# A vision block on one core: in its last stage, ACT scales the down product, POOL adds the residual and rounds the tokens, DVE multiplies the steps

## The reference, cut to what matters

```
def bitlinear(x, W, b):
    w_scale = clip(mean(abs(W)), EPS)
    Wq = clip(round(W / w_scale), -1, 1) * w_scale
    x_scale = clip(max(abs(x), axis=-1), EPS)          # one for each token
    xq = clip(round(x * (127 / x_scale)), -128, 127) * (x_scale / 127)
    return xq @ Wq.T + b
h = h + attention(layernorm(h))
h = h + bitlinear(gelu(bitlinear(layernorm(h), W1, b1)), W2, b2)
```

## Time and profile before

| what | us |
|---|---|
| median of 3 runs (354.68 to 358.23) | 355.41 |
| the profiled execution itself | 358.58 |
| its span, first to last instruction | 356.8 |
| PE busy | 310.9 (87%) |
| DVE busy | 247.1 (69%) |
| ACT busy | 214.6 (60%) |
| POOL busy | 136.8 (38%) |

### The profile page before, as it was taken

The page is one execution under the profiler, slowest core; times in us unless marked ns, Lnnn a source line. Parts: engine busy times, 40 slices in busy tenths (PEclk is TensorE's granted clock), DMA queues, the critical chain, the costliest instruction groups (busy, mean ns, idle before and its releaser), DMA issues.

```text
span 356.8 us, 9434 instructions
## 1 busy us (share of the span) xinstructions
PE 310.9 (87%) x3582; PEld 235.8 (66%) x3590; DVE 247.1 (69%) x647; ACT 214.6 (60%) x385; POOL 136.8 (38%) x262
## 2 busy tenths in 40 slices
PE   7385767999999999799799999999976899999884
PEld 6274656777777765465488778778754677776553
DVE  2616647677566736245558787788758999999982
ACT  2224445447576453344556665665635999999992
POOL 1215453556545524444392000000035566555630
PEclk9878999999999999899989999999999999999998
DMA  7952991000000000001311121221100001000011
GB/s 230 264 187 88 376 322 33 3 17 33 16 16 32 17 18 17 31 31 49 72 38 40 42 50 39 45 45 40 25 3 1 2 24 38 29 31 29 30 46 51
DMA packets 19291, 22.30 MB, mean 63 GB/s; under 512 B 2304, under 2 KB 15888, under 8 KB 19248
## 3 DMA queue, kind: packets, MB, share of 16 engines
q1 hardware_dynamic: 18544, 20.89, 19.5%
q10 hardware_dynamic: 704, 0.82, 0.9%
HBM read 16.68 MB, written 5.02 MB: 61 GB/s over the span
## 4 chain that ended last, share of the span: by engine, by line
PE 62%; DVE 19%; ACT 8%; issue 5%; DMA 3%; POOL 2%; SPq 0%; DVEq 0%; ACTq 0%
PE ps L400 14%; PE ps L443 10%; PE ps L524 9%; PE ps L547 7%; DVE sc L900 7%; PE ps L421 4%; DVE ximg L921 4%; PE ps L514 4%; PE ps L390 3%; DMA ximg<-in_x 3%; PE ps L532 3%; ACT ximg L1124 3%; PE ps L383 2%; PE ps L451 2%; ACT ximg L1119 2%
## 5 line engine op out<-in xcount | busy, mean ns | idle before, releaser
L1158 POOL TENSOR_TENSOR rs<-rs,nhalf 128x1 f32<-128x1 f32 (+1 forms) x76 | 41.7, 556 | 181.4 <-DVE rs L894 100.5
L400 PE MATMUL ps<-w_in,xT 128*128 128x256 f32 (+1 forms) x228 | 56.6, 401 | 5.8 <-ACT xT L986 5.8
L400 PEld LDWEIGHTS ps<-w_in,xT 128*128 128x128 f32 (+1 forms) x228 | 43.9, 200 | 12.9 <-ACT xT L986 6.3
L1076 ACT ACTIVATE ximg<-ps 128x296 f32<-128x296 f32 x64 | 26.6, 418 | 31.4 <-PE ps L524 30.8
L443 PE MATMUL ps<-w_qk,hnT 128*128 128x512 f32 (+1 forms) x76 | 37.3, 615 | 2.3 <-DVE h L703 2.3
L775 DVE TENSOR_TENSOR qa<-ps,tab 128x512 f32<-128x512 f32 (+1 forms) x19 | 13.1, 691 | 36.9 <-PE ps L383 36.9
L838 DVE TENSOR_REDUCE ximg<-ps 128x16 f32<-128x592 f32 x32 | 24.7, 773 | 16.5 <-PE ps L514 16.4
L524 PE MATMUL ps<-tab,ximg 128*128 128x128 f32 x256 | 35.7, 283 | 0.0
L1165 POOL TENSOR_TENSOR qa<-qa,qb 128x512 f32<-128x512 f32 (+1 forms) x19 | 24.1, 1267 | 15.6 <-DVE qb L783 15.6
L524 PEld LDWEIGHTS ps<-tab,ximg 128*128 128x128 f32 x256 | 28.1, 143 | 1.3
L986 ACT ACTIVATE xT<-ps 128x768 f32<-128x768 f32 (+1 forms) x19 | 15.0, 791 | 22.4 <-PE ps L390 18.6
(11 more groups left out here) (107 smaller groups left out, 673.8 us busy)
## 6 DMA issues: line engine op xcount, KB each, us to landing
ximg<-in_x SPq DMA_DIRECT2D x18, 384.0 KB, 8.0
ximg<-vsc SPq DMA_DIRECT2D x64, 51.0 KB, 2.0
vsc<-vt SPq DMA_DIRECT2D x18, 136.0 KB, 1.7
out<-ximg SPq DMA_DIRECT2D x18, 128.0 KB, 1.7
ximg<-in_W SPq DMA_DIRECT2D x2, 1024.0 KB, 10.5
qkT<-in_W SPq DMA_DIRECT2D x2, 384.0 KB, 6.2
wide<-in_rows SPq DMA_DIRECT2D x1, 640.0 KB, 5.5
w_qk<-in_Wqk SPq DMA_DIRECT2D x1, 512.0 KB, 8.6
```

Source lines behind the costliest of these rows:

```text
L400: pe.matmul(dst[0:n, :], xT[t % 2][:, k, 0:n], w_in[:, k, :], start=(k == 0), stop=False)
L1076: act.activation(pT[p % 2][:, g0:g0 + 4, :, :], ps_pT(b), ACT.Copy).then_inc(S[f"p_evac{b}"], 1)
L1158: pool.tensor_tensor(rs[u][0:n, i:i + 1], rs[u][0:n, i:i + 1], nhalf[0:n, :], ALU.pow).then_inc(S[done], 1)
```

## The change

Four things move in the last stage.

1. `finish` on DVE (one operation: product * step + h) is gone. ACT `rows_scaled(t)` writes product * step into `ob`, with a new semaphore e_scaled; POOL `rows_finished(t)` adds h to it in place. `down(t)` now waits for e_scaled of tile t-2.
2. `tokens_rounded` goes from ACT to POOL.
3. Both `rescale` calls go from POOL to DVE: one behind the tokens' L912, one between the hidden tile's L912 and hidden_sum.
4. The order inside POOL's step is new, and the places of the steps: rows_scaled handles tile s-6 at the end of ACT's step, rows_finished tile s-8 at the end of POOL's.

```diff
             def down(t):
                 pe.wait_ge(S["f_evac"], t + 1)
-                war(pe, "e_out", t)
+                war(pe, "e_scaled", t)
...
-            def finish(t):
...
-                v.scalar_tensor_tensor(out=ob[u][0:n, :], in0=ps_e(u)[0:n, :], scalar=sc[t % 8][0:n, 7:8],
-                                       in1=h[0:n, t, :], op0=ALU.mult, op1=ALU.add).then_inc(S["e_out"], 1)
+            def rescale(x, c, i, t):
+                v.wait_ge(S[f"{x}_xs"], t + 1)
+                n = rows(t)
+                v.tensor_scalar(sc[t % 8][0:n, c + 3:c + 4], sc[t % 8][0:n, c + 1:c + 2], wsc[0:n, i:i + 1], None,
+                                ALU.mult).then_inc(S[f"{x}_dsc"], 1)
 
             def ffn_step(s):
-                if live(s - 9, NT + 1):
-                    finish(s - 9)
                 if live(s - 3, NT + 1):
                     steps_per_unit("r", 0, s - 3)
+                    rescale("r", 0, 0, s - 3)
...
                     steps_per_unit("f", 4, s - 5)
+                    rescale("f", 4, 1, s - 5)
...
-            def tokens_rounded(t):
...
+            def rows_scaled(t):
+                u = t % 2
+                act.wait_ge(S["e_ready"], t + 1)
+                act.wait_ge(S["f_dsc"], t + 1)
+                if t >= 2:
+                    act.wait_ge(S[f"stored{u}"], 8 * (t - u))
+                n = rows(t)
+                act.activation(ob[u][0:n, :], ps_e(u)[0:n, :], ACT.Copy, scale=sc[t % 8][0:n, 7:8]
+                               ).then_inc(S["e_scaled"], 1)
...
-                if live(s, NT + 1):
-                    tokens_rounded(s)
                 if live(s - 3, NT + 1):
                     hidden_out(s - 3)
+                if live(s - 6, NT + 1):
+                    rows_scaled(s - 6)
...
+            def tokens_rounded(t):
+                pool.wait_ge(S["r_rc"], t + 1)
+                n = rows(t)
+                pool.tensor_scalar(hn[t % 2][0:n, :], hn[t % 2][0:n, :], sc[t % 8][0:n, 2:3], MAGIC, ALU.mult, ALU.add
+                                   ).then_inc(S["r_rnd"], 1)
+
+            def rows_finished(t):
+                pool.wait_ge(S["e_scaled"], t + 1)
+                pool.wait_ge(S["r_bias"], t + 1)
+                n = rows(t)
+                pool.tensor_tensor(ob[t % 2][0:n, :], ob[t % 2][0:n, :], h[0:n, t, :], ALU.add).then_inc(S["e_out"], 1)
 
             def ffn_step(s):
+                if live(s - 2, NT + 1):
+                    tokens_rounded(s - 2)
+                if live(s - 1, NT + 1):
+                    tokens_normal(s - 1)
                 if live(s - 4, NT + 1):
                     add_down_offset(s - 4)
...
+                if live(s - 8, NT + 1):
+                    rows_finished(s - 8)
```

More of the change, by code:

```diff
@@ L195, in vit_block @@
             "m_set z_ready r_sum r_stat r_aggr r_var r_rstd r_nmr r_norm r_amax r_xs r_rc r_dsc r_rnd r_bias n_turned "
-            "n_evac f_ready f_sum f_gelu f_amax f_xs f_rc f_dsc f_rnd f_turned f_evac e_ready e_out "
+            "n_evac f_ready f_sum f_gelu f_amax f_xs f_rc f_dsc f_rnd f_turned f_evac e_ready e_scaled e_out "
             "stored0 stored1"
@@ L959, in ffn_step @@
                     step_size("r", 0, s - 2)
-            for s in range(NT + 10):
+            for s in range(NT + 6):
                 ffn_step(s)
@@ L1101, in _ @@
             act.wait_ge(S["m_set"], 1)
-            def tokens_rounded(t):
-                act.wait_ge(S["r_rc"], t + 1)
+            def rows_scaled(t):
[4 more added lines that the diff above has]
+                    act.wait_ge(S[f"stored{u}"], 8 * (t - u))
                 n = rows(t)
-                act.activation(hn[t % 2][0:n, :], hn[t % 2][0:n, :], ACT.Identity, bias=magic[0:n, :],
-                               scale=sc[t % 8][0:n, 2:3]).then_inc(S["r_rnd"], 1)
+                act.activation(ob[u][0:n, :], ps_e(u)[0:n, :], ACT.Copy, scale=sc[t % 8][0:n, 7:8]
+                               ).then_inc(S["e_scaled"], 1)
             def n_out(t):
@@ L1140, in ffn_step @@
                     n_out(s - 1)
-                if live(s, NT + 1):
-                    tokens_rounded(s)
                 if live(s - 3, NT + 1):
                     hidden_out(s - 3)
-            for s in range(NT + 4):
+                if live(s - 6, NT + 1):
+                    rows_scaled(s - 6)
+            for s in range(NT + 7):
                 ffn_step(s)
@@ L1248, in tokens_normal @@
                                    ALU.mult, ALU.add).then_inc(S["r_norm"], 1)
-            def rescale(x, c, i, t):
-                pool.wait_ge(S[f"{x}_xs"], t + 1)
+            def tokens_rounded(t):
+                pool.wait_ge(S["r_rc"], t + 1)
                 n = rows(t)
-                pool.tensor_scalar(sc[t % 8][0:n, c + 3:c + 4], sc[t % 8][0:n, c + 1:c + 2], wsc[0:n, i:i + 1], 1.0,
-                                   ALU.mult, ALU.mult).then_inc(S[f"{x}_dsc"], 1)
+                pool.tensor_scalar(hn[t % 2][0:n, :], hn[t % 2][0:n, :], sc[t % 8][0:n, 2:3], MAGIC, ALU.mult, ALU.add
[5 more added lines that the diff above has]
+                pool.tensor_tensor(ob[t % 2][0:n, :], ob[t % 2][0:n, :], h[0:n, t, :], ALU.add).then_inc(S["e_out"], 1)
             def ffn_step(s):
+                if live(s - 2, NT + 1):
+                    tokens_rounded(s - 2)
+                if live(s - 1, NT + 1):
+                    tokens_normal(s - 1)
                 if live(s - 4, NT + 1):
                     add_down_offset(s - 4)
[L1259 to L1262, removed]
                 if live(s, NT + 1):
                     inverse_root(3, s, s % 2, "r_var", "r_rstd")
-                if live(s, NT + 1):
                     token_shift(s)
-                if live(s - 1, NT + 1):
-                    rescale("r", 0, 0, s - 1)
-            for s in range(NT + 8):
+                if live(s - 8, NT + 1):
+                    rows_finished(s - 8)
+            for s in range(NT + 9):
                 ffn_step(s)
```

## The result

The changed kernel takes 361.68 us (median of 4 runs, 360.83 to 363.15), the kernel before 355.22 us in the runs beside it (median of 4): ratio 1.017, 95% interval 1.011 to 1.023. Measured again twice, with 5 or 6 runs of it and more of the kernel before, it took 362.97 against 357.43 (1.016, 1.010 to 1.022) and 363.20 against 357.50 (1.018, 1.015 to 1.021). A few runs of some kernels were slowed; ratios and their intervals leave these out. The change costs some 6 us, 5.5 to 5.7 in the larger sets; I had said 3.8. The direction and the main links of the forecast stand, its size was too small, and the first median lies 0.1 us above the upper end of my range (355.41 times the ratio is 361.45, just inside it).

A forecast was written before the change was run, and what follows sets the result against it. A closed DVE-ACT chain of waits, 4.14 us a turn, was taken to bound the last stage. Turns +1.44 and +0.36 and the end +2.0 gave +3.8 us: 359.2 us, range 356.8 to 361.6.

The forecast's parts named there:

- What bounds the stage: Last stage: a closed chain of DVE and ACT waits limits each turn (hidden L900 to the next), 4.14 us before the change.
- the loop: L900, L912, L921 on DVE, gelu on ACT, next L900: 4.14 us a turn, 4.26 with the added L927.
- DVE's own sum: DVE's work per turn: 4.18 us before, 3.79 without L932, 4.03 with two L927, below the chain's 4.26.
- L932 lies outside this loop: Taking L932 (0.39 us) off DVE gives back at best 0.04 us a turn, 0.4 us in all.
- The price of L927: Between the hidden tile's L912 and L921, the added DVE operation costs 0.12 us every turn; ends 0.07 and 0.20.
- Turns: The 18 turns from first to last hidden L900: +1.44 us for 15 and +0.36 for the last three.
- Rival C: L927 paid in full at 0.20 us, and lower PE clock delays turn_hidden(18) by 0.7: +5.9, 361.3 us; chance 0.18.
- A: Rival: the added L927 is nearly free at 0.07 us, sum +2.9, 358.3 us; chance 0.22.
- ACT and POOL: ACT's sum falls 0.12 us a turn, worth nothing; POOL's work rises to 3.3 of 4.26 us, costed at nothing.
- The end: Stage end: ACT's order makes down(17) wait for rows_scaled(15), ACT and POOL finish instead of DVE: last sum +2.0 us.
- the two chains: Stage end: held last products on PE, and stores freeing ob[0] for tile 18; both put the last sum at 356.4 us.
- within 1%: Outcome within 3.6 us of the kernel before, chance 0.39; slower 0.58, faster 0.03.

The follow-up runs named there:

- step behind the sum: The changed kernel with the hidden tile's L927 put behind hidden_sum (L921) instead of ahead of it: 361.6 us, +4.1 to the kernel before.
- both parts undone: The changed kernel with the hidden tile's L927 behind hidden_sum and tiles 15 to 18 finished by DVE: 357.89 us against 357.45, ratio 1.0000.
- the step twice: The changed kernel with a second operation like L927, result unused, between the hidden tile's L927 and L921: 365.77 us, +8.3 to the kernel before.
- the rounding on POOL: The kernel before with only tokens_rounded moved from ACT to POOL: 358.34 us against 357.50, ratio 1.0037.
- the last four tiles on DVE: The changed kernel with tiles 15 to 18 finished by DVE in one operation, as before: 360.10 us, ratio 1.0064 to the kernel before.

## Why the prediction was right, and where it was short

*What bounds the stage.* Right for the changed kernel: DVE stands free for 0.13 us ahead of L900, one operation out of the loop gives 1.9 us back, one more in it costs 1.9. But DVE's own sum was wrong: I had 3.79 without L932 and 4.03 with the two L927, and the rows give 3.79 + 0.12 = 3.91 and 4.12. I had left out the wait between L906 and L912 that L932 had covered. The loop was the limit by 0.13 us, not by the 0.23 that I had.

"L932 lies outside this loop" rests on the first turns of the kernel before, which last 4.13 to 4.14 with DVE waiting for gelu. No experiment took L932 away and put nothing in its place. In the kernel with the step behind the sum and in the one with both parts undone the turn is 4.16, against 4.17 before, but DVE's own sum is 4.16 there too: what L932 left (0.39) was taken up nearly whole by the two L927 (0.12 each) and the wait (0.12). So the gain of 0.04 us a turn at best wasn't tested by itself.

*The price of L927.* Right. I took 0.12 from two rows of other operations; the rows say 0.11 from start to start and 0.19 to 0.20 in duration, and it is the same with two of them (0.11 and 0.13). Turns: forecast +1.8, measured +1.75. That they agree so well is partly luck, as the next paragraph shows. The sentence on the "DRAIN" in the Trainium skill's page "VectorE: DVE Perf Modes", section "The DRAIN you can't avoid", taken by itself, would have had 0.20 for each; the same paragraph goes on that a next operation that is not held starts earlier. The rows agree with the second sentence: where the operation behind L927 had nothing to wait for, it started 0.06 to 0.09 us before the end of L927. I had left that sentence out of the prediction. Rival C loses that half, and A (0.07) falls as well.

One turn took 4.51 and not 4.25: L921 started 0.37 us behind L927 there instead of 0.11, with nothing to wait for that the profile shows.

```profile
298.62 1.28 DVE L921 SCALAR_TENSOR_TENSOR ximg<-ps,sc,wide 128x1024 f32<-128x1024 f32 x1 [0.17 <-issue]
```

It was the same turn in all five profiles of kernels with this order on DVE, but not in the one with the step twice. I had no such term; it is 0.26 us, and its cause is open. Without it the turns grew by 1.49 us: 0.08 to 0.11 each, since my 0.12 was a little high and the middle turns of before were already at 4.17.

*ACT and POOL.* Right: 74.33 with the rounding on POOL, and no turn was held by POOL. The fill, from the first residual sum to the first hidden L900, went from 9.75 to 9.81 us.

*The end.* The mechanism was right in each of its links: down(16) held by rows_scaled(14), down(17) by rows_scaled(15) behind hidden_out(18), rows_scaled(17) by a store. rows_scaled(18) waited for its product (0.77 us) in the profile of the changed kernel, and for a store only where the products ran at the full clock (0.19, step behind the sum); I had the two chains end together. In the profile it was +2.2 (9.86 against 7.65) for a forecast of +2.0, the products having taken 3.71 us and not 3.33. With the last four tiles on DVE it was gone, at the same clock.

*The term that was mis-sized* is nevertheless this one. I compared with one execution of before, whose end ran mostly at the lower clock. Where all tiles are finished on DVE, the end follows the clock: 7.65, 7.27 and 6.11 us, for two products in 3.33, 3.22 and 2.04 us (the last is the kernel with the rounding on POOL). The changed kernel took 9.86, 9.86 and 9.85 at the lower clock, and where its variant ran at the full clock it was still 9.32, for the stores hold it. (With the last four tiles on DVE it was 7.64 at the lower clock and, with both parts undone, 7.14 at the full one, held by a store.) I had written "So even at the full clock the end does not come earlier" and had not drawn from it that the kernel before does. So the end costs 2.2 us with both at the lower clock, 3.2 with both at the full one, 3.7 if only the changed kernel is at the lower one, and not 2.0. To this comes a last store that took longer from issue to landing, 2.3 to 2.6 us instead of 2.0, which I had put at nothing. Two rows of the DMA list, before and after:

```profile
out<-ximg SPq DMA_DIRECT2D x1, 64.0 KB, 2.0
```

```profile
out<-ximg SPq DMA_DIRECT2D x1, 64.0 KB, 2.6
```

Together: 1.75 + (2.2 to 3.7) + (0.3 to 0.6) = 4.3 to 6.1 us, for 5.5, 5.7 and, in the first and smallest set, 6.5 (6.0 by the ratio) measured.

*The chances.* I gave a third of the forecast's 0.50 to "within 1%" and then added 0.12 for it; a third is 0.17.

*What stays open.* Neither of the two profiles of before ran its end at the full clock throughout, and how often that happens in executions without a profile isn't known, so the 5.7 is made plausible by this sum, not shown. The place at which the stage starts scatters from 260.8 to 265.8 us over twelve profiles. The kernel with the rounding on POOL was slower by 0.2 to 2.4 us though its stage was not longer. So up to about 1 us ahead of the stage may belong to some of these kernels. The kernel with both parts undone speaks against it. What the record does show is that the scatter goes with the mean granted clock: the 12 executions of before with 0.979 or more took 355.8 us on average, the 20 with 0.969 to 0.972 took 358.5. The changed kernel's 15 had 0.966 on average, the 61 of before 0.974. Part of that is its longer end at the lower clock, and how much of it lies ahead of the stage was not separated.

## What to carry to other kernels

Two engines that are both full can still be waiting for each other tile by tile: look for the chain that closes on itself, and price an added operation by whether it lies in that chain, not by which engine has room. Work taken from outside the chain gives nothing (0.49 us a turn off ACT here), a one-element operation put into it costs its 0.11 us each time, and the cure is to put it behind the operation that others wait for. An operation also covers the wait of the next one for the one ahead: what its removal frees on its engine is less than its length by that wait (0.39 less 0.12 here). When one step is split over two engines, check the last tiles by hand: a program in fixed order puts the first buffer release behind the last tile's other work, and a two-buffer output then waits for its own stores.

## What the hardware showed that I had not expected

- The clock at the end differs between executions: 3.33 and 3.22 us for the same last 16 matmuls in two of the kernel before, and 2.03 to 3.71 us over kernels that differ in one or two operations. For kernels that finish on DVE that made up to 1.5 us of the end (7.65 and 6.11). That two executions of one program differ by as much was not seen. The row of granted clock shows it, here for the changed kernel in its third profile and for the one with the rounding on POOL (third number from the end):

```profile
354.00:356.00 2.00, 2.00 (x10) 1.24 (x8) 0.00 (x0) 0.47 (x1) 0.43 (x1) 0.50 0.39 131
```

```profile
351.00:353.00 2.00, 2.00 (x21) 1.65 (x19) 0.48 (x1) 0.69 (x1) 0.00 (x0) 1.00 0.23 79
```

- The loads at the start scatter: the second group of L739 on DVE started at 10.06 us in one profile and at 8.91 in another, and the first residual sum anywhere in a range of 5 us; that the one makes the other was not shown. The stretch of 18 turns repeats to 0.02 us between profiles of kernels with the same order, so a change of a stage is better read there than in the medians of a few runs.
- POOL's tensor_scalar with one per-partition scalar and one constant (L1252) took 0.48 us, that with two per-partition scalars (L1246) 0.55, both on 128 x 256.
